# Seven block products in place of eight for the gate and up products of one feature chunk, over pairs of token steps

## The reference, cut to what matters

```
gate = x @ W_gate.T + 0.5 * lora      up = x @ W_up.T + 0.5 * lora      (1376 features each)
down = (silu(gate) * up) @ W_down.T + 0.5 * lora
x    = x + down @ sign(W).T + bias0
x    = x + (low-rank map by adapter id)(x) @ (W + low rank).T + bias1
```

## Time and profile before

| | |
|---|---|
| three runs | 893.63, 895.05, 895.05 us, median 895.05 |
| profiled execution | 894.13 us, span 892.3 us |
| instructions | 22052 in the trace, 7564 of them matmuls |
| granted TensorE clock, mean | 1.00 of full speed |
| bytes moved | 137.33 MB, mean 154 GB/s |

### The profile page before, as it was taken

One profiled execution on the slowest core, in us unless ns is written; L12 is line 12 of the kernel. 1 busy time (PEld: TensorE's weight loads), 2 busy tenths in 40 slices (PEclk: granted clock), 3 DMA queues, 4 the chain that ended last, 5 costly groups with the idle time before them and its releaser, 6 DMA issues.

```text
span 892.3 us, 22052 instructions
## 1 busy us (share of the span) xinstructions
PE 886.9 (99%) x7564; PEld 731.0 (82%) x7564; DVE 411.4 (46%) x986; ACT 203.7 (23%) x381; POOL 122.4 (14%) x141
## 2 busy tenths in 40 slices
PE   9999999999999999999999999999999999999998
PEld 6888888888888888888888888888888888888886
DVE  5854444444344544435354453444444344444444
ACT  4852212112121221212122221121222212122120
POOL 0200111011111111011111001111101111110111
PEclk9999999999999999999999999999999999999999
DMA  9934464554555555555555555555555455555553
GB/s 346 418 114 131 130 167 125 152 145 133 161 135 154 134 150 149 130 160 142 153 129 150 150 141 145 151 143 138 148 152 143 136 157 138 154 136 149 148 128 91
DMA packets 148947, 137.33 MB, mean 154 GB/s; under 512 B 54848, under 2 KB 120384, under 8 KB 148800
## 3 DMA queue, kind: packets, MB, share of 16 engines
q1 hardware_dynamic: 91744, 111.11, 43.2%
q10 hardware_dynamic: 56240, 22.83, 9.9%
q0 software_dynamic: 944, 3.15, 0.9%
HBM read 94.80 MB, written 11.01 MB: 119 GB/s over the span
## 4 chain that ended last, share of the span: by engine, by line
PE 98%; DVE 1%; DMA 0%; ACT 0%; issue 0%; SPq 0%; DVEq 0%
PE gu_ps L859 57%; PE y_ps L896 27%; PE out_ps L918 3%; PE gu_ps L1004 3%; PE out_ps L969 2%; PE gu_ps L995 1%; PE out_ps L905 1%; PE y_ps L859 1%; PE out_ps L859 1%; PE gu_ps L896 1%; PE out_ps L926 1%; DMA lb_raw<-in_lbw 0%; DVE a_lo L645 0%; PE gu_ps L1033 0%; DVE weff_raw L791 0%; PE y_ps L973 0%
## 5 line engine op out<-in xcount | busy, mean ns | idle before, releaser
L859 PE MATMUL gu_ps<-wu_sb,xT_sb 128*128 128x432 f32 (+1 forms) x1152 | 261.3, 371 | 0.0
L859 PE MATMUL gu_ps<-wg_sb,xT_sb 128*128 128x432 f32 (+1 forms) x1152 | 254.5, 370 | 0.5 <-DVE act_all L663 0.5
L896 PE MATMUL y_ps<-down_sb,actT_sb 128*128 128x512 f32 x1023 | 241.5, 393 | 0.0
L896 PEld LDWEIGHTS y_ps<-down_sb,actT_sb 128*128 128x128 f32 x1023 | 189.6, 188 | 60.2 <-issue 21.4
L859 PEld LDWEIGHTS gu_ps<-wg_sb,xT_sb 128*128 128x128 f32 x1152 | 216.3, 188 | 25.9 <-DVE xT_sb L645 1.4
L859 PEld LDWEIGHTS gu_ps<-wu_sb,xT_sb 128*128 128x128 f32 x1152 | 214.1, 188 | 21.4
L645 DVE TENSOR_TENSOR actT_sb<-landed,actT_sb 128x512 fp32r<-128x512 f32 (+1 forms) x96 | 60.9, 635 | 191.9 <-ACT actT_sb L480 191.8
L480 ACT CAST actT_sb<-landed 128x512 fp32r<-128x512 f32 (+1 forms) x96 | 56.1, 585 | 309.4 <-DMA landed<-act_all 194.0
L439 POOL TENSOR_TENSOR x_in<-x_in,bias_sb 128x512 f32<-128x512 f32 x32 | 41.2, 1287 | 615.9 <-DMA x_in<-in_x 615.9
L645 DVE TENSOR_TENSOR xT_sb<-xT_raw,xT_sb 128x512 fp32r<-128x512 f32 x32 | 22.1, 692 | 105.3 <-ACT xT_sb L480 105.3
L677 DVE TENSOR_TENSOR t_own<-out_ps,const_sb 128x64 f32<-128x64 f32 x32 | 7.2, 225 | 135.5 <-PE out_ps L918 133.0
(11 more groups left out here) (128 smaller groups left out, 557.5 us busy)
## 6 DMA issues: line engine op xcount, KB each, us to landing
b_rows<-in_btab SPq DMA_DIRECT2D x128, 236.0 KB, 3.1
a_raw<-in_atab SPq DMA_DIRECT2D x128, 152.0 KB, 2.3
landed<-act_all SPq DMA_DIRECT2D x132, 64.0 KB, 2.1
xT_raw<-in_xT SPq DMA_DIRECT2D x32, 256.0 KB, 2.6
x_in<-in_x SPq DMA_DIRECT2D x32, 256.0 KB, 2.8
landed<-act_all ACTq DMA_DIRECT2D x124, 64.0 KB, 2.2
out_x<-out_sb SPq DMA_DIRECT2D x31, 256.0 KB, 2.9
x_landed<-x_turn ACTq DMA_DIRECT2D x122, 64.0 KB, 2.2
```

The costliest lines, as they stand in the source:

```text
L859: last = nc.tensor.matmul(o, w, m, start=start and n == 0, stop=stop and n == len(terms) - 1, skip_group_check=not check)
L896: last = nc.tensor.matmul(to[:], actT_sb[:, ACTT_SLOT[c] + n, a, :], down_sb[:, blk, b, :], start=begin and (c, n) == (0, 0) and (a, b) == ...
```

## The change

The 512-feature chunk c1 of gate and up is a product of a token block by [input halves] by [gate, up]. For a pair j of steps (tokens of step 2j: x0, of step 2j+1: x1, each in two halves a and b of 256 inputs) this is a 2 by 2 by 2 block product with eight block products of 6 matmuls. From pair 1 on it is done with seven, by the Strassen-Winograd scheme. The sums on the input side (s1 to s4, 256 wide) are made by DVE and split by ACT and DVE. The sums on the weight side (T1 to T4, each 2 x 512 columns) are made once by POOL, split, and stored in DRAM as `t_table`. On the product side DVE adds u2, u4, up_even, up_odd and gate_odd (512 wide each, with PSUM). Steps 0 and 1 still do c1 with eight block products.

The core of the diff, shortened:

```diff
+            def mid(bank, x_parts, w, signal, start):
+                product(gu_ps[bank][:], [(x_parts(k, a), w[:, b, k, :]) for k in range(HALF) for a, b in THREE], signal,
+                        start=start, check=False)
+            def p6(g, j):
+                pe.wait_ge(L["act_done"], g * NC)
+                pe.wait_ge(L["s_lo"], nth(S_SPLIT, "s2", j))
+                slot_ready(1, 2 * j - 1)
+                mid(2, s_of(1), slot_sb[1], L["mid_mm"], True)
+            def p3(g, j):
+                pe.wait_ge(L["mid_sum"], nth(MID_SUM, "u4", j))
+                pe.wait_ge(L["s_lo"], nth(S_SPLIT, "s4", j))
+                mid(1, s_of(0), w22_sb, L["mid_mm"], False)
...
 # POOL
+            def load_even(g, j):
+                pool.wait_ge(L["mid_mm"], nth(MID_MM, "p5", j))
+                end_bias1(g)
+                load_t(4, L["slot1_in"])
+                load_t(3, L["slot0_in"])
+            def load_odd(g, j):
+                pool.wait_ge(L["mid_mm"], nth(MID_MM, "p4", j))
+                end_bias1(g)
+                load_t(1, L["slot0_in"])
+                load_t(2, L["slot1_in"])
+            difference(t1_raw, t3_raw, t1_raw)      # then T3, T2, T4, 128x1024 each
...
 # SP, ahead of step 0
-            sp.wait_ge(S["sbd_mm"], 2)
             rows_stored(sp)
+            load_xT(1, 1)
+            sp.wait_ge(S["down_mm"], NBLK)
             load_b(0)
-            sp.wait_ge(S["down_mm"], NBLK)
+            sp.dma_start(t3_raw[:], wmid[:, KC:KC + HALF]).then_inc(S["raw1_in"], 16)
+            ... t1_raw, t2_raw, t4_raw
...
 # DVE step
+                if seven(j):
+                    even_products(g, j, prev) or odd_products(g, j, prev)   # by parity
                 turn_t(g)
...
+                if first(g):
+                    dve.wait_ge(S["t_raw"], t_count(2))
+                    low_t(1)
+                    low_t(3)
                 if nxt is not None:
-                    split_xT(nxt)
+                    split_xT(nxt, 1 - parity)
...
                 for c in range(NC):
                     gated(g, c)
                     turn_act(g, c)
-                split_actT(g, 0)
+                if parity == 1 and nxt is not None:
+                    first_sums(j + 1)
+                    low_s(1, j + 1)
+                    low_s(2, j + 1)
                 if prev is not None:
                     add_y(prev)
                     turn_x1(prev)
+                split_actT(g, 0)
                 split_actT(g, 1)
-                split_actT(g, 2)
```

More of the change, by code:

```diff
@@ L554, in step, with finish @@
                     send_x1(act, prev)
+                if first(g):
+                    act.wait_ge(S["t1_out"], 32)
+                    high_t(2)
+                    act.wait_ge(S["t3_out"], 32)
+                    high_t(4)
+            def finish(g):
                 split_actT(g, 2)
-            def finish(g):
                 act.wait_ge(E["x1_tr"], 1)
@@ L850, in _ @@
-            step(G - 1, G - 2, G - 3, None)
+            for r in range(4):
+                nc.vector.tensor_copy(act_all[group(r), F:FP], ident[group(r), group(r)]).then_inc(S["pad_set"], 1)
+            dve.wait_ge(S["pad_set"], 4)
+            step(0, 0, 0, None, None, 1)
+            step(1, 0, 1, 0, None, 2)
+            step(2, 1, 0, 1, 0, 3)
+            step(3, 1, 1, 2, 1, 4)
+            with dve.Fori(2, G // 2 - 1) as j:
+                step(2 * j, j, 0, 2 * j - 1, 2 * j - 2, 2 * j + 1)
+                step(2 * j + 1, j, 1, 2 * j, 2 * j - 1, 2 * j + 2)
@@ L878, in up, with side @@
[L878 to L886 removed]
+            def side(x_at, w, w_at):
+                return [(x_at[:, k, a, :], w[:, b, k, w_at]) for k in range(KC) for a, b in THREE]
@@ new lines, in gate, with up @@
+            def gate(g, c):
+                w = CHUNKS[c][1]
+                if c == 0:
+                    if first(g):
+                        pe.wait_ge(S["wg_lo"], KC)
+                    pe.wait_ge(L["xT_lo"], g + 1)
+                if not first(g):
+                    pe.wait_ge(L["act_done"], g * NC - NC + c + 1)
+                product(gu_ps[GU_BANK[c][0]][:, 0:w], side(xT_sb, wg_sb, slice(SIDE_AT[c], SIDE_AT[c] + w)), None)
+            def up(g, c):
+                w = CHUNKS[c][1]
+                if c == 0 and first(g):
+                    pe.wait_ge(S["wu_lo"], KC)
+                product(gu_ps[GU_BANK[c][1]][:, 0:w], side(xT_sb, wu_sb, slice(SIDE_AT[c], SIDE_AT[c] + w)),
+                        L["xT_used"] if c == 2 else None)
@@ new lines, in eight, with gate_mid, up_mid @@
+            def eight(g, bank, halves):
+                product(gu_ps[bank][:], [(xT_sb[:, k, a, :], halves[k // HALF][:, b, k % HALF, :])
+                                         for k in range(KC) for a, b in THREE], None)
+            def gate_mid(g):
+                if first(g):
+                    pe.wait_ge(S["wmid_lo"], nth(MID_SPLIT, "w21"))
+                else:
+                    pe.wait_ge(L["act_done"], g * NC - NC + 2)
+                eight(g, 0, (w11_sb, w21_sb))
+            def up_mid(g):
+                if first(g):
+                    pe.wait_ge(S["wmid_lo"], nth(MID_SPLIT, "w22"))
+                eight(g, 1, (w12_sb, w22_sb))
```

582 lines of the change are left out of this document (416 added, 166 removed).

## The result

The changed kernel takes 978.08 us (median; 975.63 to 980.17) against 895.05 us (893.63 to 895.25) for the kernel before on the same chip: ratio 1.0927, 95% interval 1.0914 to 1.094. It is 83 us slower where 11.5 us faster was forecast, and outside the forecast's range.

A forecast was written before the change was run, and what follows sets the result against it. TensorE, busy 99%, was taken to bound the kernel alone; 20.7 us saved less 4.2 for b, 3.0 at the start and 2.0 at the end gave -11.5 us, so 883.5 us median, range 875 to 900.

The forecast's parts named there:

- 90 matmuls by 0.23 us, intervals of 23.1 and 27.2 us: TensorE in pairs 1 to 15: 6 matmuls fewer per pair, 20.7 us saved; odd steps last 23.1 us, even ones 27.2.
- No wait at p6, p3, lora_ready, small_ready: TensorE's waits in the loop: spare 3 us, 1.3, 0.9 (thin) and 1.4, so no cost.
- Rival 2: DVE chain late in every pair, at p3 or turn_t: 7.5 us more, 891 us; chance 0.13.
- b_in in odd steps: Wait for b ahead of odd steps' low-rank rows: 0.9 us left, T1/T2 load beside b, 4.2 us in all, ends 0 and 13.
- Rival 1: T1/T2 load goes ahead of b in every odd step: worst 1.9 us a step, 27 us, 906 us; chance 0.17.
- Start, 3.0 us: T blocks' sums and low parts delay gate c0 of step 1: 3.0 us taken, least 0, 4 if POOL is slower.
- the forecast's own 75.2: Forecast start of gate c0 of step 1, against 73.41 before, called 1.9 us late.
- End, 2.0 us: Last group's down waits for chunk 0's low part, made behind add_y and turn_x1: 2.0 us, ends 0 and 2.5.
- The sum: Whole kernel: -20.7 + 4.2 + 3.0 + 2.0 = -11.5 us, 882.6 us for the profiled execution, 883.5 us median.
- 14 x 50.3: Loop: pairs were to repeat in 50.3 us with no wait, 50.6 with the forecast's wait for b.

The follow-up runs named there:

- experiments 9: Changed kernel with the T1/T2 loads of odd steps on SP's queue behind b's four transfers instead of POOL's: 896.99 us, ratio 1.0028 to the kernel before.
- 10: As experiments 9, plus raw T loads ahead of load_b(0) and split_actT(31, 0) ahead of add_y in the last step: 887.39 us, ratio 0.9936 to the kernel before.
- experiment 12: Changed kernel with six small POOL additions before the T1/T2 loads of odd steps, issuing them later on POOL's queue: 909.87 us, ratio 1.0181 to the kernel before.
- experiment 4: Changed kernel with 20 unused matmuls ahead of lora_ready in odd steps from pair 1, keeping TensorE busy: 965.08 us, ratio 1.0781 to the kernel before.

## Why the prediction was wrong

- *90 matmuls by 0.23 us, intervals of 23.1 and 27.2 us.* Right: 7474 matmuls, 23.2 and 27.3 us wherever nothing waited, in the changed kernel and in experiments 9, 10 and 12.
- *No wait at p6, p3, lora_ready, small_ready.* Right in the loop: DVE, busy 56% for 46%, is on time. Rival 2 did not happen.
- ***b_in in odd steps: "I take 0.3 us in each of the 14 odd steps".*** This is the step that failed. The timetable in it was right: the fourth b transfer was to be issued 0.8 us behind the end of `small`, and is (433.5 for 432.72); the rows were due 4.8 us behind the end of `small`, and up c2 ends there. The size of the T load was right too: 18.4% of 978.3 us for 70.26 MB are 5.4 us for 2.1 MB, for 5.3. Wrong was the landing: 9.2 us, where I let the rows of before bound it at 4.9 us. Those rows hold no bulk load that another queue issues beside b; I took the crowded prologue for one, but POOL's queue, where T now goes, moved next to nothing there (3.15 MB over the whole span). Nor is the 4.9 us the prologue's: the view of b_rows there (44 to 48 us, DMA share 1.0) has 3.6 to 4.1 us, and the 4.9 is the fourth transfer of step 1, issued at 82.48 with no bulk load beside it. Rival 1 had the mechanism, with a chance of 0.17. Its worst, b landing near 8 us behind the start of `small`, was to be 1.9 us a step; b landed at 11.3 and the wait was 5.2 us there, 4.3 on the mean.
- *What a wait costs.* Missing altogether. I priced a wait by its length, and behind it the clock stood at 0.50 (443 to 447 us in the step shown): 29.9 us on top of 56.5, and in experiment 4, without the idle time, the same instructions take their full-clock time again. With both, rival 1 is 86 us instead of 27.
- *Start, 3.0 us.* Wrong in size: gate c0 of step 1 starts at 80.46, not at 75 to 77 (the forecast's own 75.2 is 1.8 us behind 73.41, not 1.9), and `small` of step 2 waits 4.0 us for x1, whose add_y waited for an x_in that landed 7.8 us after its issue beside the first T1/T2 load: the failed step's mechanism once more. The view of t_raw at the start:

```profile
L559 POOL TENSOR_TENSOR t_raw<-t_raw x4: 2358/2385/3377, 67.3 to 74.7; 128x1024 f32<-128x1024 f32 x4
...
L843 DVE TENSOR_TENSOR t_lo<-t_raw,t_high_lo x2: 1225/2294/3362, 74.7 to 75.8; 128x1024 fp32r<-128x1024 f32 x2
...
DMA to landing us min/median/max: 5.0/6.8/8.1
```

  The first difference starts at 67.3 rather than 63.6, since the raw loads need 5.0 to 8.1 us behind b and not 3.3: 3.7 us. The differences take 2.4 us each for my 2.6, which gives a little back. And DVE's second low part takes 3.36 us, not 1.23, beside POOL's fourth difference (3.38 for 2.36): 2.1 us.
- *End, 2.0 us.* Right: TensorE waits 2.0 us for DVE's low part, the last of the waits shown above, and not at all when the edit is undone.
- *The sum.* With the T1/T2 load on b's queue and the raw loads first, the same seven products give a span of 884.3 us, 3.5 us above the forecast's 880.8. That closeness is part luck: the 880.8 hold 4.2 us for b and 2.0 us for the end, which that run does not pay, so that like for like it is 9.7 us above. Its loop takes 707.3 us where the forecast has 14 x 50.3 = 704; most of the difference lies ahead of step 3. The arithmetic of what TensorE does held in the loop; the sum failed on one landing and on the clock behind it (86.4 us in the loop), and start and end, 5.0 us in the forecast and 3.6 net of pair 1's gain, were 17.4 us net.

## What to carry to other kernels

A bulk load issued beside small transfers that a tight wait needs is priced by when they land with it, not by its share of the bytes; where no row of the profile has the two side by side, the upper bound is the whole load, at every step. Issue it behind their last issue, by more than some tenths of a microsecond: here that alone was 978 against 910 us from POOL's queue and 897 us from b's own, and then look at what the load meets next. And here each wait of some 4 us on a TensorE that was never idle cost over half as much again in clock, so a small slack that is used up in every step of a loop deserves more than a chance of 0.17.

## What the runs showed of the hardware

- Small transfers issued shortly before or during a 2 x 1 MB load of another queue landed late, the last of them at about the end of that load: b 9.2 us for 3.1 (442.7, T2 at 442.9), x_in 7.8 and 8.4, x1 8.5 for 2.2. Issued ahead of it by 0.7 us or more they were clear of it: 3.7 to 3.9 us in experiment 12, and 3.3 to 4.0 us in the even steps from 6 on of the changed kernel, where T4/T3 follow b's last issue by 1.4 to 2.8 us. Why the later load's packets go first no run here shows.
- The Trainium skill, "DMA: Bandwidth & Descriptors", "Issuing engines are not separate DMA queues", says that transfers of all issuing engines share the same DMA engines, and that the choice of the issuing engine saves only the time of the issue. Nothing here speaks clearly against it: 897 against 910 us (experiments 9 and 12) goes with a different distance between the issues.
- Behind waits of 4.3 us on the mean (the longest 5.3) TensorE's granted clock was 0.50 from 443 to 447 us in the step shown, and such stretches cost 2.3 us a time; with 4.7 us of filling matmuls in its place it stayed at 0.993 over the span.
- A 1024-wide subtraction of DVE with two operands in SBUF took 3.36 us for 1.23 (75.84 to 79.20) beside one of POOL, which took 3.38 us for 2.36 (74.74 to 78.12). With DVE's subtraction before it (74.69, 1.23 us) the three would take 4.8 us one after the other, and took 4.5: next to nothing of them overlapped.
